# Attention of layer 0 by halves of the queries: maxima head by head in three PSUM banks, values in groups of four units

## The reference, cut to what matters

```
q, k, v = heads(x @ Wq + bq), heads(x @ Wk + bk), heads(x @ Wv + bv)
attn = einsum('bqd,bkd->bqk', q, k) / sqrt(HD)
attn = attn + rel_bias_h[..., :, None] + rel_bias_w[..., None, :]   # from q and rel_h, rel_w
attn = softmax(attn, axis=-1)
out = einsum('bqk,bkd->bqd', attn, v)          # then out @ Wp + bp
```

## Time and profile before

| | us |
|---|---|
| median of 3 runs | 3546.41 (3543.08 to 3547.0) |
| the profiled execution | 3543.45 |
| its span | 3541.7 |
| TensorE busy | 3325.4 (94%) |
| VectorE busy | 1638.0 (46%) |
| ScalarE busy | 1197.0 (34%) |
| GpSimd busy | 1089.1 (31%) |

### The profile page before, as it was taken

One profiled execution on the slowest core, in us unless ns is written; L12 is line 12 of the kernel. 1 busy time (PEld: TensorE's weight loads), 2 busy tenths in 40 slices (PEclk: granted clock), 3 DMA queues, 4 the chain that ended last, 5 costly groups with the idle time before them and its releaser, 6 DMA issues.

```text
span 3541.7 us, 49223 instructions
## 1 busy us (share of the span) xinstructions
PE 3325.4 (94%) x21388; PEld 2384.5 (67%) x21388; DVE 1638.0 (46%) x1496; ACT 1197.0 (34%) x1301; POOL 1089.1 (31%) x618
## 2 busy tenths in 40 slices
PE   8988899999998889999999888999999988899999
PEld 6854458776785455877678544587767854458776
DVE  5346535435434653543543465344354345634434
ACT  3334432133334443213332444321323244432132
POOL 0036570024003666003300466600330046660032
PEclk9999999999999999999999999999999999999999
DMA  3210013104311001311431100131043110013113
GB/s 126 81 36 19 13 30 116 36 28 140 116 69 27 19 16 34 109 36 34 148 108 62 28 19 18 36 113 36 28 148 119 49 30 16 19 43 106 36 31 104
DMA packets 158709, 210.95 MB, mean 60 GB/s; under 512 B 110496, under 2 KB 110752, under 8 KB 158496
## 3 DMA queue, kind: packets, MB, share of 16 engines
q1 hardware_dynamic: 158496, 207.81, 18.9%
HBM read 132.26 MB, written 50.33 MB: 52 GB/s over the span
## 4 chain that ended last, share of the span: by engine, by line
PE 67%; DVE 15%; issue 7%; ACT 5%; SPq 3%; DMA 2%; POOL 1%; ACTq 0%; DVEq 0%; POOLq 0%
PE score L912 14%; PE score L913 12%; PE score L914 12%; PE head_out L1042 7%; DVE max_part L687 6%; PE mx L977 6%; PE score L1012 4%; PE mx L980 3%; SPq L336 3%; DVE recip L716 3%; PE mx L995 2%; DVE o_raw L721 2%; ACT b_lo_raw L486 1%; DMA recip<-recip 1%; DVE b_lo L707 1%
## 5 line engine op out<-in xcount | busy, mean ns | idle before, releaser
L444 POOL TENSOR_TENSOR acc<-acc,prob 128x1024 f32<-128x1024 f32 x288 | 721.5, 2530 | 243.9 <-ACT prob L584 243.7
L584 ACT ACTIVATE prob<-score 128x1024 f32<-128x1024 f32 (+3 forms) x576 | 515.2, 908 | 646.1 <-PE score L1025 548.1
L687 DVE TENSOR_REDUCE max_part<-mx 128x2 f32<-128x1024 f32 x384 | 467.5, 1218 | 424.8 <-PE mx L980 424.8
L1042 PE MATMUL head_out<-prob,v 128*64 128x512 f32 (+4 forms) x2496 | 492.0, 519 | 0.0
L912 PE MATMUL score<-a_hi,w_hi 128*128 128x512 f32 x1152 | 461.8, 401 | 18.0 <-DVE w_lo L628 6.2
L913 PE MATMUL score<-a_lo,w_hi 128*128 128x512 f32 x1152 | 449.9, 391 | 0.0
L914 PE MATMUL score<-a_hi,w_lo 128*128 128x512 f32 x1152 | 449.1, 390 | 0.0
L444 POOL TENSOR_TENSOR acc<-prob 128x1024 f32<-128x1024 f32 x48 | 113.5, 2389 | 970.7 <-ACT prob L584 782.2
L977 PE MATMUL mx<-k_hi,q_hi 64*128 64x512 f32 (+2 forms) x1152 | 266.3, 453 | 125.0 <-DVE max_part L687 109.8
L912 PE MATMUL score<-w_hi,a_hi 128*128 128x256 f32 x1152 | 346.3, 301 | 0.0
L977 PEld LDWEIGHTS mx<-k_hi,q_hi 64*128 64x128 f32 x1152 | 115.4, 185 | 317.5 <-issue 276.6
(11 more groups left out here) (107 smaller groups left out, 5436.9 us busy)
## 6 DMA issues: line engine op xcount, KB each, us to landing
raw<-weights SPq DMA_DIRECT2D x96, 768.0 KB, 4.2
g_mem<-g SPq DMA_DIRECT2D x24, 1024.0 KB, 4.6
recip<-recip SPq DMA_DIRECT2D x384, 64.0 KB, 2.0
xin<-x_t SPq DMA_DIRECT2D x24, 512.0 KB, 6.2
xr<-x_t SPq DMA_DIRECT2D x24, 512.0 KB, 5.1
x_mem<-xr SPq DMA_DIRECT2D x24, 512.0 KB, 7.0
xr<-x_mem SPq DMA_DIRECT2D x24, 512.0 KB, 5.3
y_t<-xr SPq DMA_DIRECT2D x24, 512.0 KB, 5.2
```

The costliest lines, as they stand in the source:

```text
L444: nc.gpsimd.tensor_tensor(acc[:, :, a:b], with_, now, ALU.add).then_inc(added, 1)
L584: nc.scalar.activation(prob[:, ug % P_SLOTS, :, 0:b - a], score[:, u % 2, :, 0:b - a], ACT.Exp, scale=SCALE).then_inc(prob_ok, 1)
L687: nc.vector.reduce_max(max_part[:, t, part, :], mx[:, :, 0:b - a], AX.X).then_inc(max_ok, 1)
L1042: last = nc.tensor.matmul(head_out[rows_of(h), half, x - half * HALF:y - half * HALF], v[:, t, p * 128 + 64 * h:p * 128 + 64 * h + 64], pr ...
```

## The change

In attention of layer 0 the units go through all key tiles for the first half of the queries, then for the second. Values need one bank then (bank 3 of `lot`, the four banks that were `mx` and `head_out`), and the maxima of pairs 1 to 5 use the other three in turn, one per head: head h of maximum n lies in bank (2n + h) % 3. VectorE reduces each head by an instruction of its own, with a semaphore `half_max_ok`, and TensorE waits for the first head of the last maximum only. Values are made in fours. Sums, reciprocals, spreads, normalisation and the split of the output come by halves. The maxima run up to two ahead into the pair after next, and the bias has four sets of buffers, the fourth in the second weight slot, so the ninth weight chunk is loaded in pair 2 and split in pair 5. The order of steps by units is new on all engines. Layer 1 does the same steps in the same order.

```diff
+PARTS = (2, 1)
+GROUPED = 4
-SETS = 3
+SET_OF = ([0, 3, 2, 0, 1, 2], [0, 1, 2, 0, 1, 2])
     if layer == 0:
-        return u // 2, u % 2 * HALF, (u % 2 + 1) * HALF
+        return u % QT, u // QT * HALF, (u // QT + 1) * HALF
+BEFORE = [1, 1, 0] + [1] * 7 + [0, 1, 1, 0, 1, 1]
+BEFORE_FIRST = [1] * 13 + [0, 1, 1]
+BEHIND = [u in (1, 5, 9) for u in range(2 * QT)]
-V_MAX = ([54 + int(4.5 * k) for k in range(2 * QT)],
+V_MAX = ([20 + int(4.5 * k) for k in range(2 * QT)],
-V_SHIFT = (V_MAX[0][-1] + 8, 34)
+V_SHIFT = (V_MAX[0][-1] + 12, 34)
...
@@ sync, attention of layer 0
+                    if 0 < p < PAIRS - 2:
                         load_bias(f, p + 2)
+                    if p:
+                        spread(f, p - 1, 1)
+                    if p == 2:
+                        sp.wait_ge(score_ok, unit_no(f, 1, 2 * QT - 1))
+                        weights(f, 9)
+                    spread(f, p, 0)
@@ scalar: behind the exponential of unit u of pair p, layer 0
+  u == 1 and p: out_copy(f, p - 1, 1); sums_copy(f, p - 1, 1)
+  u == 4 and p: out_hi(f, p - 1, 0)
+  u == 5 and ahead: bias_turn(f, p + 2, 0)
+  u in (5, 13) and p == LAST: weight_hi(f, QK_CHUNKS + V_CHUNKS + u // 8)
+  u == 8 and p: out_hi(f, p - 1, 1)
+  u == 9: if ahead: bias_turn(f, p + 2, 1); then sums_copy(f, p, 0)
+  u == 11: out_copy(f, p, 0)
+  u == 13: if ahead: bias_first(f, p + 2); if p < LAST: bias_hi(f, p + 1)
@@ vector
+            def head_maximum(f, n):
+                p, k = n // (2 * QT) + 1, n % (2 * QT)
+                t, part, _, _ = max_at(0, k)
+                n += f // 2 * LAST * 2 * QT
+                dve.wait_ge(max_mm, unit_no(f, p, k))
+                for h in range(2):
+                    nc.vector.reduce_max(max_part[:, t, part, h:h + 1], lot[:, (2 * n + h) % 3, :], AX.X)\
+                        .then_inc(half_max_ok, 1)
+                    for u in range(UNITS[0]):
+                        before, behind = maxima_around(p, u)
+                        for n in before:
+                            head_maximum(f, n)
+                        if p < LAST and u == 13:
+                            shift(f, p + 1)
+                            bias_lo(f, p + 1)
+                        for n in behind:
+                            head_maximum(f, n)
+                        if u == 1 and p:
+                            normalise(f, p - 1, 0)
+                        if u == 2 and p:
+                            invert(f, p - 1, 1)
+                        if u in (5, 13) and p == LAST:
+                            weight_lo(f, QK_CHUNKS + V_CHUNKS + u // 8)
+                        if u == 7 and p:
+                            normalise(f, p - 1, 1)
+                        if u == 9 and p:
+                            out_lo(f, p - 1, 0)
+                            out_lo(f, p - 1, 1)
+                        if u == 10:
+                            invert(f, p, 0)
@@ tensor
+            def head_maximum(f, n, sums_before):
...
+                banks_free(sums_before)
+                pe.wait_ge(max_ok, maxima_issued[0])
+                if n:
+                    pe.wait_ge(half_max_ok, 2 * n - 1)
+                maximum_product((2 * n % 3, (2 * n + 1) % 3), f, p, k)
+                        before, behind = maxima_around(p, u)
+                        for n in before:
+                            head_maximum(f, n, int(u in (2, 10)))
+                        scores(f, p, u)
+                        for n in behind:
+                            head_maximum(f, n, 0)
+                        if u == 13 and p < LAST:
                             shift(f, p + 1)
+                        if u % GROUPED == 1 and u > 1:
+                            for e in range(u - GROUPED - 1, u - 1):
+                                values(f, p, e)
+                            if u == 9:
+                                sums(f, p, 0)
+                        elif u == 1 and p:
+                            for e in range(2 * QT - GROUPED, 2 * QT):
+                                values(f, p - 1, e)
+                            sums(f, p - 1, 1)
```

More of the change, by code:

```diff
@@ L125, in pair_no, with part_no, last_part, recips_before @@
     return f * PAIRS + p + 1
+def part_no(f, p, h):
+    return sum(PAIRS * PARTS[g % 2] for g in range(f)) + p * PARTS[f % 2] + h + 1
+def last_part(f, p):
+    return part_no(f, p, PARTS[f % 2] - 1)
+def recips_before(f, p, h):
+    return 2 * PAIRS * f + 2 * p + h
+def columns_of(f, h):
+    return slice(h * HALF, (h + 1) * HALF) if f % 2 == 0 else slice(0, TOKENS)
 def bias_loaded(f, p):
-    before = f // 2 * (128 + 16 * (p % SETS == 0))
-    return before + 128 + 16 if f % 2 else before + (p // SETS + 1) * 64
+    s = SET_OF[f % 2][p]
+    before = f // 2 * SET_LOADS[s]
+    return before + SET_LOADS[0] if f % 2 else before + 64 * SET_OF[0][:p + 1].count(s)
 def first_no(f, p):
@@ L433, in _ @@
                         before = adds_before(f, p)
+                        if layer == 0:
+                            h, t = u // QT, u % QT
+                            if t == 0:
+                                continue
+                            gp.wait_ge(prob_ok, ug + 1)
+                            if t == 1 and (f or p):
+                                gp.wait_ge(sum_mm, part_no(f, p - 1, h) if p else last_part(f - 1, LAST))
+                            if t > 1:
+                                gp.wait_ge(added, before + h * (QT - 1) + t - 1)
+                            with_ = prob[:, (ug - 1) % P_SLOTS, :, :] if t == 1 else acc[:, :, a:b]
+                            nc.gpsimd.tensor_tensor(acc[:, :, a:b], with_, now, ALU.add).then_inc(added, 1)
+                            continue
                         if u < 2:
@@ L436, in _ @@
                         gp.wait_ge(prob_ok, ug + 1)
[L437 to L438 removed]
+                        if u == 2:
+                            gp.wait_ge(sum_mm, part_no(f, p, 0) - 1)
                         if u > 3:
[L440 removed]
+                            gp.wait_ge(added, before + u - 2)
                         old = prob[:, (ug - 2) % P_SLOTS, :, :]
[L442 to L445 removed]
                         done = [unit_at(1, e)[1:] for e in range(u)]
@@ L553, in _ @@
                         weight_hi(f, j // 2 + 2)
+                    if layer == 0 and j == 8:
+                        bias_turn(f, 0, 0)
+                        bias_turn(f, 0, 1)
+                        bias_first(f, 0)
                     if layer == 1 and j == 2:
@@ L567, in _ @@
                                              ACT.Copy).then_inc(v_ok, 1)
-                        if n == 0 and layer == 0:
-                            bias_first(f, 0)
                         if n == 2:
@@ L573, in _ @@
                             weight_hi(f, QK_CHUNKS + 2)
-                        if n == VN - 2 and layer == 0:
-                            bias_hi(f, 0)
+                        if layer == 0:
+                            if n == VN - 6:
+                                bias_hi(f, 0)
+                            if n == VN - 5:
+                                bias_turn(f, 1, 0)
+                            if n == VN - 4:
+                                bias_turn(f, 1, 1)
+                            if n == VN - 3:
+                                bias_first(f, 1)
                 for p in range(PAIRS):
@@ L852, in _ @@
+                if layer == 0:
+                    normalise(f, LAST, 0)
+                    invert(f, LAST, 1)
+                    out_lo(f, LAST, 0)
+                    normalise(f, LAST, 1)
+                    out_lo(f, LAST, 1)
+                else:
+                    normalise(f, LAST - 1, 0)
+                    out_lo(f, LAST - 1, 0)
+                    invert(f, LAST, 0)
+                    normalise(f, LAST, 0)
+                    out_lo(f, LAST, 0)
                 if layer == 1 and nx < PHASES:
@@ L1001, in scores @@
             def scores(f, p, u):
-                layer, s, slot = f % 2, p % SETS, u % 2
+                layer, s, slot = f % 2, SET_OF[f % 2][p], u % 2
                 t, a, b = unit_at(layer, u)
@@ L1158, in _ @@
                 last_pair = PAIRS - 1
-                values(f, last_pair, UNITS[layer] - 2)
-                values(f, last_pair, UNITS[layer] - 1)
+                for u in range(UNITS[layer] - (2 if layer else GROUPED), UNITS[layer]):
+                    values(f, last_pair, u)
                 def output(n, c):
```

413 lines of the change are left out of this document (228 added, 185 removed).

## The result

The changed kernel takes 3397.05 us (median of 4 runs, 3393.11 to 3407.57) against 3545.86 us for the kernel before in the same comparison (4 runs, 3543.08 to 3547.0): the ratio is 0.9589, 95% interval 0.9571 to 0.9606, so 4.1% faster. The forecast was 3382, the range 3350 to 3440. The profiled execution took 3393.11 us, its span is 3391.3; it is 14.5 us longer than the 3378.6 forecast for it.

What follows compares the result with a forecast made beforehand. TensorE, stalled by VectorE's maximum reductions, was taken as the bound. Pairs of 44.2, 3 x 47.3, 45.0 and 39.5 gave 270.6 us an image against 314.6; net 41.2 saved, 165 in all: 3382 us, range 3350 to 3440.

Steps and rivals of the forecast that it cites:

- The bound and the mechanism: Layer 0 attention: TensorE bounds; releasing a maximum after one head's reduction cuts maximum to maximum from 2.14 to 1.61 us.
- VectorE becomes the bound: Rival, 0.05: one-bank passes cost about 1.22 us, a steady pair takes 57 us, total 3550 us and more.
- change its name: Rival, 0.05: scores keep ScalarE's or GpSimd's pace through five probability slots; pairs stay near 54 us, total 3535 to 3550.
- The work of a pair: TensorE's work in a steady pair without stalls: scores 18.4, maxima 7.4, values 15.2, sums 1.1, shift 1.9, together 44.0 us.
- (1): Steady pair, after the first values: VectorE's reciprocal waits for the copy of the sums, so unit 4 stalls 0.5 us.
- (3): Steady pair: the second reciprocal, behind unit 10 on VectorE, stalls unit 12 by 0.5 us.
- (2): Steady pair: the half normalisation, 1.4 us, stands ahead of unit 8's passes on VectorE; unit 9 stalls 1.0 us.
- (4): Steady pair, unit 13: exponential, bias_first, bias_hi, then b_lo at 1.22 us ahead of unit 14's reductions; unit 15's maximum stalls 1.4.
- The dear chain: Rival, 0.28: b_lo falls on GpSimd's adds in most pairs, takes 2.56 us, unit 15 stalls 2.5, clock falls: 3425 us.
- Covered, unless VectorE's denser passes slow them by a third: GpSimd's 14 adds a pair, 34.9 us of 47.3, were expected to cause no stall.
- Around it: Outside the pairs, per image: value projection +2.2 us, one more clock drop +1.6, wait before the last sums -1.0.
- The signs: Expected afterwards: 640 passes of 0.65 to 0.72 us, steady pairs 46 to 49, reduction wait about a third, last pairs 39 to 40.

Runs made afterwards that it cites:

- the combined kernel: Changed kernel with second-half normalisation behind unit 9, both bias steps before unit 13's exponential, projection maxima from group 27, pair 5's first sums behind unit 12: 3319.11 us.
- The test by bias_first alone: Changed kernel with bias_first one exponential earlier on ScalarE, behind unit 12's instead of unit 13's: 3393.71 us, ratio 0.9579 to the kernel before.

## Why the prediction was right, and where its sizes were off

**The bound and the mechanism: right.** Taking the release by the first head away gives back 133 of 149 us.

**The pass.** 0.69 from the line through 622 and 1218 ns, measured 681 ns, two back to back 1.27 to 1.29 (estimate 1.27). "VectorE becomes the bound" needed 1.2 us. The wait did not only change its name either: the exponentials' wait for a slot costs TensorE nothing that shows in a steady pair. By the formula of the Trainium skill (VectorE: DVE Perf Modes, The TRN2 errata), which I weighed in the prediction, a pass would be 658 ns; the trace is 23 ns above it. The advice there for large tiles is given for sources in SBUF; for PSUM the section has only the formula.

**The work of a pair.** 44.0 us forecast; 47.71 less stalls of 3.4 is 44.3, and the combined kernel, in which only the two stalls of 0.13 are left, has 44.32. A run of 16 value records is 3.58 as at the end of pair 5, the two halves of the sums 0.57 each.

**The stalls: 3.3 forecast (the four terms as written sum to 3.4), 3.4 measured, but not the same ones.** So the length of a steady pair came out by luck in part: 47.3 forecast, 47.7 measured. (1) and (3), the reciprocals: 0.5 each, measured 0.13. (2), the half normalisation: this is the mis-sized term. I took 1.4, "half of a pass beside a busy GpSimd". It measured 2.37 and stalls unit 9 by 1.77, not 1.0. Half the columns halve only the pass's own part, 1.08 to 0.55 us; what comes before is the rest of the add, whose length the pass has no share in. The rows that showed it stood in the trace before: 56 ends at the same distance. I had read 2.56 and 2.46 as durations and never put GpSimd's line beside them. (4), b_lo ahead of unit 15: forecast 1.4, measured 1.38, by luck. I had the add end as b_lo starts and the pass at 1.22. It starts 4.2 us after the shift, as I had it (4.3), but 0.6 us before the add's end, and takes 1.68. Behind it, only one head's reduction stands ahead of the maximum: 0.75 us from b_lo's end to unit 15's maximum, where I had 1.3. The two errors, +0.46 and -0.5, cancel. The test by bias_first alone shows that what counts there is the add's end, not b_lo's start.

**The dear chain,** the rival with 0.28, assumed the right thing, that b_lo falls on an add in most pairs: 20 of 24 do. Its price was wrong. A pass that is issued in an add's last 0.6 us takes 1.68, not 2.56, and the stall stays under 2 us.

**Pairs 0 and 4** came to 44.76 and 44.99 (44.2 and 45.0 forecast).

**Pair 5: 39.5 forecast, 41.45 in images 0 and 2, 43.0 in images 1 and 3.** A wait I did not see, and a term that the sum put at nothing. The sums of its first half are asked for behind unit 9, and GpSimd isn't done, because VectorE's passes hold it up as it does them: four adds take 11.79 us, not 9.6. TensorE, GpSimd, and VectorE:
```profile
464.06 3.65 PE L1212 MATMUL lot<-prob,v 128*64 128x512 f32 x16
469.84 0.64 PE L1229 MATMUL lot<-acc,ones 128*32 128x256 f32 x8 [2.12 <-POOL acc L515]
```
```profile
457.99 11.79 POOL L515 TENSOR_TENSOR acc<-acc,prob 128x1024 f32<-128x1024 f32 x4
```
```profile
459.03 2.96 DVE L747 TENSOR_TENSOR w_lo<-raw,w_hi 128x1536 fp32r<-128x1536 f32 x1 [6.36 <-ACT w_hi L552]
461.92 2.89 DVE L856 TENSOR_TENSOR o_raw<-o_raw,recip 128x512 f32<-128x512 f32 x1
464.74 5.60 DVE L863 SCALAR_TENSOR_TENSOR q_lo<-o_raw,bv,q_hi 128x512 fp32r<-128x512 f32 x2
```
The four adds take 2.38, 3.75, 2.63 and 2.60 us. The one of 3.75 begins at 460.52, during w_lo, the longest of VectorE's passes here and one that the change itself has put into pair 5 (the split of a weight chunk at unit 5). That pass alone accounts for some 1.4 of the 2.2 us. In images 1 and 3 the clock falls to 1.2 GHz behind this wait, for a record of 3.4 us. "Covered, unless VectorE's denser passes slow them by a third" had the mechanism in it, and I had dismissed it on the average over a pair; locally the adds are slowed by 23%, and that is enough where a wait stands right behind them.

**Around it.** The value projection became 3.0 us longer in image 0 and 3.3 to 3.5 in the others, not 2.2: two stalls of 1.5 to 1.7, of which I had seen only the first. The second is the low part of the last weights, at group 74, ahead of a reduction. The wait before the last sums went as foreseen, 1.4 where I had 1.0. Of clock falls I had one more an image, 6.4 us; there are seven fewer in all.

**The sum.** Attention 1100.47 against 4 x 270.6 = 1082.4, 18.1 more: per image 0.6 in pair 0, 1.25 in the three steady pairs together, 1.95 to 3.5 in pair 5. The value projection took 13.2 where I had 8.8, 4.4 more, and the output projection gave 7.1 where I had 4.0, which takes 3.1 off: 19.4. The miss is 14.5. The 4.9 between are within the 6.4 that I had set down for clock falls and that didn't come.

**The signs.** Passes of 681 ns, 640 of them, and values at 3.58 came as named. Three signs did not: TensorE's wait for reductions (nearly half, not a third; the four stalls that I had summed come to more than a third themselves), the largest wait of a pair (ahead of unit 9, not 15) and the last pairs (41.45 to 43.0, not 39 to 40). Of the signs of being wrong, the last, adds of GpSimd that end the waits, came in part: they end four of TensorE's waits by name, and hold up the VectorE passes behind the two large stalls of a pair.

## What to carry to other kernels

When a pass of VectorE over SBUF has two durations in a trace, put the other engine's timeline beside it and compare ends. If the end keeps a fixed distance to the end of a GpSimd instruction, the price is the rest of that instruction and about the pass's own time: smaller tiles on VectorE help little; issuing the pass before the GpSimd instruction, or where the matmuls don't wait behind it, gave all or most of the stall back here (1.5 and 1.6 us a steady pair). A release by halves can decide whether a restructuring pays at all: take it back on its own and time that. And an edit's stalls can't be added to a fixed list: moving one block of work uncovers or covers the stall of another.

## What the runs showed of the hardware

The distance between the end of a GpSimd add and that of a VectorE pass with two inputs in SBUF that began during it, in the attention of layer 0 before and after: 1.08 to 1.09 us for 1024 columns in all 76 cases, 0.55 to 0.56 for 512 columns in all 32. The weights' low part, 1536 columns, has 1.61 to 1.62 in all 16. In o_raw and b_lo that is 0.13 to 0.14 shorter than the pass alone (1.22 and 0.68), in w_lo likewise (1.75), in q_lo of 1024 columns 0.20 (1.28); my reading, not shown, is that some of the pass's own start lies beside the add. The other way round, an add that falls on a pass is lengthened (2.52 for 2.40, 1.72 for 1.29). Two adds of 512 columns take 2.67 us where one of 1024 takes 2.45.
